# Correlation of pixels with their neighbours: the high parts multiplied in one direction, from a half-scaled tile that VectorE writes

## The reference, cut to what matters

```python
def conv_ref(feature, w, b):
    norm = sqrt(sum(feature * feature, axis=1, keepdims=True))
    fn = feature / maximum(norm, 1e-12)
    fp = pad(fn, 2 pixels of zeros on each side of H and W)
    sims = [sum(fp[:, :, r:r+32, c:c+32] * fn, axis=1) for c in range(5) for r in range(5)]
    cat = concatenate([feature, stack(sims, axis=1)], axis=1)      # 512 + 25 channels
    return relu(einsum('bihw,oi->bohw', cat, w) + b)

x = x + conv_ref(group_norm(x, 32 groups), w0, b0)
x = x + conv_ref(group_norm(x, 32 groups), w1, b1)
```

## Time and profile before

| | before |
|---|---|
| time, median of 3 runs (lowest to highest) | 539.54 us (538.83 to 540.25) |
| span of the profiled execution, first to last instruction | 538.4 us |
| own time of the profiled execution outside its span | not listed apart |
| busy: PE / PEld / DVE / ACT / POOL | 490.8 / 278.2 / 350.5 / 278.6 / 131.8 us |
| mean granted TensorE clock | 0.981 of full speed |

### The profile page before, as it was taken

How to read it: one execution, slowest core, us unless ns; L and a number is a source line. 1 busy time by engine, 2 the same in 40 slices (tenths; PEclk the granted TensorE clock), 3 DMA queues, 4 the chain that set the end, 5 groups by cost and what they waited for, 6 DMA issues and landing times.

```text
span 538.4 us, 7705 instructions
## 1 busy us (share of the span) xinstructions
PE 490.8 (91%) x2824; PEld 278.2 (52%) x2824; DVE 350.5 (65%) x820; ACT 278.6 (52%) x370; POOL 131.8 (24%) x189
## 2 busy tenths in 40 slices
PE   0658699489998999999999999999999999999996
PEld 0535355354644646464645556464646455564442
DVE  4788794767869296958758595858677676433322
ACT  1352544575394656647393757556473938433222
POOL 3453511040521313131220404040313112040400
PEclk9989799789999999999999999999999999999999
DMA  8282444441332716494957625042332326362332
GB/s 295 99 270 67 129 165 133 133 134 38 94 92 74 219 49 211 149 309 131 321 165 254 212 102 161 15 129 47 98 89 75 110 79 185 138 203 90 126 126 114
DMA packets 58547, 75.81 MB, mean 141 GB/s; under 512 B 11764, under 2 KB 45612, under 8 KB 58510
## 3 DMA queue, kind: packets, MB, share of 16 engines
q1 hardware_dynamic: 48718, 66.40, 36.7%
q0 software_dynamic: 9792, 8.92, 7.0%
HBM read 34.97 MB, written 37.79 MB: 135 GB/s over the span
## 4 chain that ended last, share of the span: by engine, by line
PE 77%; DVE 10%; ACT 4%; DMA 4%; POOL 2%; SPq 2%; issue 2%; DVEq 0%; ACTq 0%
PE conv_ps L530 56%; PE gram_ps L470 14%; PE conv_ps L539 5%; DVE stats L759 3%; POOL v L432 2%; DVE opnd L808 2%; DMA xs<-in_x_dram 1%; ACT opnd L627 1%; PE turn_ps L520 1%; ACT v L633 1%; DVE wmax L858 1%; ACT act_out L662 1%; DMA skew<-band_dram 1%; DMA band_dram<-band 1%; DVE xs L886 1%
## 5 line engine op out<-in xcount | busy, mean ns | idle before, releaser
L530 PE MATMUL conv_ps<-opnd,wh 128*128 128x512 f16 x512 | 194.9, 381 | 1.2 <-DVE wl L874 1.2
L530 PE MATMUL conv_ps<-opnd,whh 128*128 128x512 f16 x512 | 194.7, 380 | 0.0
L530 PE MATMUL conv_ps<-opnd,wl 128*128 128x512 f16 x512 | 194.7, 380 | 0.0
L662 ACT ACTIVATE act_out<-conv_ps,bias,wdown 128x512 f32<-128x512 f32 x128 | 96.4, 775 | 141.0 <-PE conv_ps L539 129.1
L886 DVE TENSOR_TENSOR xs<-xs,act_out 128x512 f32<-128x512 f32 x128 | 87.7, 696 | 50.8 <-ACT act_out L662 50.2
L470 PE MATMUL gram_ps<-opnd 128*128 128x256 f16 (+1 forms) x960 | 105.0, 269 | 3.4 <-ACT band L643 3.4
L470 PEld LDWEIGHTS gram_ps<-opnd 128*128 128x128 f16 x960 | 91.1, 100 | 16.6 <-ACT band L643 3.7
L808 DVE SCALAR_TENSOR_TENSOR opnd<-opnd,v 128x1024 f16<-128x1024 f16 x64 | 78.4, 1235 | 28.7 <-ACT v L633 21.3
L627 ACT ACTIVATE opnd<-xs,affine 128x1024 f16<-128x1024 f32 x64 | 78.8, 1238 | 17.4 <-DVE affine L802 17.4
L759 DVE BATCH_NORM_STATS2 stats<-xs 128x6 f32<-128x512 f32 x128 | 79.9, 681 | 5.6 <-DMA xs<-in_x_dram 5.6
L530 PEld LDWEIGHTS conv_ps<-opnd,whh 128*128 128x128 f16 x512 | 50.0, 98 | 61.2 <-issue 1.0
(11 more groups left out here) (77 smaller groups left out, 238.6 us busy)
## 6 DMA issues: line engine op xcount, KB each, us to landing
xs<-in_x_dram SPq DMA_DIRECT2D x32, 512.0 KB, 6.4
band_dram<-band SPq DMA_DIRECT2D x64, 256.0 KB, 2.9
out_dram<-xs SPq DMA_DIRECT2D x32, 512.0 KB, 2.9
skew<-band_dram SPq DMA_DIRECT2D x32, 266.0 KB, 3.5
vol<-corr_h POOLq DMA_DIRECT2D x48, 50.0 KB, 2.7
rows_dram<-rows SPq DMA_DIRECT2D x32, 65.8 KB
rows_dram<-rows SPq DMA_DIRECT2D x32, 63.3 KB
mirror<-rows_dram POOLq DMA_DIRECT2D x14, 110.9 KB, 2.6
```

What stands on the lines that cost most here:

```text
L530: pe.matmul(conv_ps[:, g % 4, :], w[:, l, t, m * P:(m + 1) * P], opnd[:, u % RING, part, t, n * HALF:(n + 1) * HALF], start=(t == 0 and w ...
L662: act.activation(act_out[:, g % 2, :], conv_ps[:, g % 4, :], ACT.Relu, bias=bias[:, l, m:m + 1], scale=wdown[:, l, m:m + 1]).then_inc(relu, 1)
```

## The change

The low part is kept single: the second pass writes v (`exact_tile`, `exact_tiles`), and DVE subtracts h from it. `whh` and `half_weights` are gone; the single low part meets `wh` in the convolution, and the doubling of the affine factors (L802) is gone. For the high parts, DVE writes a new tile `half` for each unit: for each block its own 128 columns times 0.5, and the 64 columns of the next two rows unscaled (`half_tile`: two instructions a tile, one of 8 x 128 and one of 7 x 64 f16 elements). PE multiplies a block's highs with these 192 columns (128 for the last block), while the lows still run over all rows from two above to two below; the mirrored sum supplies the rows above and the missing half. The order of the two parts in a sum is swapped, lows first. There is one `half`, so writing it waits until the products of the unit before are done (`gram`). The products wait for `halved` in place of `high`. In the slots the halves of tiles 0 and 1 stand behind low tile 1, those of tiles 2 and 3 directly behind their low tile; for unit 3 the first two stand behind `neighbours(2)`.

```diff
-        whh = sb("whh", [P, LAYERS, KT, C], F16)
-        v2 = sb("v2", [P, 2, PIX], F32)
+        v = sb("v", [P, 2, PIX], F32)
+        half = sb("half", [P, KT, BLOCKS, AHEAD], F16)      # AHEAD = (ROWS + R) * WI = 192
...
             def product(u, j, t, part):
                 p, h = j // 2, j % 2
-                r0 = max(ROWS * j - R, 0)
-                r1 = min(ROWS * (j + 1) + R, HI)
+                top = ROWS * j - (R if part else 0)
+                r0, r1 = max(top, 0), min(ROWS * (j + 1) + R, HI)
                 at = h * BAND + (r0 - (ROWS * j - R)) * WI
-                return pe.matmul(gram_at(u, p)[:, at:at + (r1 - r0) * WI],
-                                 opnd[:, u % RING, 0, t, j * P:(j + 1) * P],
-                                 opnd[:, u % RING, part, t, r0 * WI:r1 * WI],
-                                 start=(t == 0 and part == 0 and (u > 0 or h == 0)),
-                                 stop=(t == KT - 1 and part == 1 and (u > 0 or h == 1)))
+                size = (r1 - r0) * WI
+                moving = opnd[:, u % RING, 1, t, r0 * WI:r1 * WI] if part else half[:, t, j, 0:size]
+                return pe.matmul(gram_at(u, p)[:, at:at + size], opnd[:, u % RING, 0, t, j * P:(j + 1) * P], moving,
+                                 start=(t == 0 and part == 1 and (u > 0 or h == 0)),
+                                 stop=(t == KT - 1 and part == 0 and (u > 0 or h == 1)))
...
             def products(u, p):
                 if p == 0:
-                    pe.wait_ge(high, KT * (u + 1))
                     pe.wait_ge(low, KT * (u + 1))
+                    pe.wait_ge(halved, 2 * KT * (u + 1))
...
-                    for w, part in ((wh, 0), (wl, 0), (whh, 1)):
+                    for w, part in ((wh, 0), (wl, 0), (wh, 1)):
...
-                dve.wait_ge(gn_step, base + 10)
-                dve.tensor_scalar(affine[:, 1, :, :], affine[:, 0, :, :], 2.0, None, ALU.mult).then_inc(gn_step, 1)
...
             def low_tile(u, t):
                 dve.wait_ge(high, KT * u + t + 1)
-                dve.wait_ge(twice, KT * u + t + 1)
-                dve.scalar_tensor_tensor(out=opnd[:, u % RING, 1, t, :], in0=opnd[:, u % RING, 0, t, :], scalar=-2.0,
-                                         in1=v2[:, t % 2, :], op0=ALU.mult, op1=ALU.add).then_inc(low, 1)
+                dve.wait_ge(exact, KT * u + t + 1)
+                dve.tensor_tensor(opnd[:, u % RING, 1, t, :], v[:, t % 2, :], opnd[:, u % RING, 0, t, :], ALU.subtract
+                                  ).then_inc(low, 1)
+
+            def half_tile(u, t):
+                h = opnd[:, u % RING, 0, t, :].rearrange("p (j n) -> p j n", n=P)
+                wait(dve, gram, PAIRS * u)
+                dve.tensor_scalar(half[:, t, :, 0:P], h, 0.5, None, ALU.mult).then_inc(halved, 1)
+                dve.tensor_copy(half[:, t, 0:BLOCKS - 1, P:AHEAD], h[:, 1:BLOCKS, 0:AHEAD - P]).then_inc(halved, 1)
...
             for t in range(KT):
                 low_tile(0, t)
+                half_tile(0, t)
...
             low_tile(3, 1)
             correlation(1)
             neighbours(2)
+            half_tile(3, 0)
+            half_tile(3, 1)
             low_tile(3, 2)
+            half_tile(3, 2)
             low_tile(3, 3)
+            half_tile(3, 3)
...
                 if valid(k + 1):
                     low_tile(k + 1, 0)
                     low_tile(k + 1, 1)
+                    half_tile(k + 1, 0)
+                    half_tile(k + 1, 1)
                 for j in range(GROUPS):
...
                     if j in (1, 2) and valid(k + 1):
                         low_tile(k + 1, j + 1)
+                        half_tile(k + 1, j + 1)
```

More of the change, by code:

```diff
@@ L70, in build @@
     PAIRS = BLOCKS // 2
+    AHEAD = (ROWS + R) * WI
     REACH = 2 * R * WI + S
@@ L146, in build @@
         gtmp = sb("gtmp", [P, KT], F32)
-        affine = sb("affine", [P, 2, 2, KT], F32)
+        affine = sb("affine", [P, 2, KT], F32)
         nsq = sb("nsq", [P, BLOCKS], F32)
@@ L184, in build @@
         high = sem("high")
-        twice = sem("twice")
+        exact = sem("exact")
         low = sem("low")
+        halved = sem("halved")
         gram = sem("gram")
@@ L418, in scaled_weights, with exact_tiles @@
                                        ALU.mult, ALU.mult).then_inc(w_scaled, 1)
[L420 to L427, removed]
+            def exact_tiles(u, tiles):
                 pool.wait_ge(gn_step, GN_STEPS * (u + 1))
@@ L431, in double_tiles @@
                     wait(pool, low, KT * u + t - 1)
[L432 to L436, removed]
+                    pool.tensor_scalar(v[:, t % 2, :], xs[:, ring_slot(unit_batch(u)), t, :],
+                                       affine[:, 0, t:t + 1], affine[:, 1, t:t + 1], ALU.mult, ALU.add
+                                       ).then_inc(exact, 1)
+            exact_tiles(0, range(KT))
             scaled_weights(0)
-            half_weights(0)
-            double_tiles(1, range(KT))
+            exact_tiles(1, range(KT))
             volume_in(pool, 0)
-            double_tiles(2, range(KT))
+            exact_tiles(2, range(KT))
             volume_in(pool, 1)
             for k in range(EARLY, UNITS):
-                if k == W1_SLOT:
-                    half_weights(1)
                 views_from_dram(pool, k)
@@ L466, in product @@
                 p, h = j // 2, j % 2
[L467 to L468 removed]
+                top = ROWS * j - (R if part else 0)
+                r0, r1 = max(top, 0), min(ROWS * (j + 1) + R, HI)
                 at = h * BAND + (r0 - (ROWS * j - R)) * WI
[L470 to L474 removed]
+                size = (r1 - r0) * WI
[3 more added lines that the diff above has]
+                                 stop=(t == KT - 1 and part == 0 and (u > 0 or h == 1)))
             def first_products():
                 for t in range(KT):
[L479 removed]
                     pe.wait_ge(low, t + 1)
+                    pe.wait_ge(halved, 2 * (t + 1))
                     for p in range(PAIRS):
                         for j in (2 * p, 2 * p + 1):
[L483 removed]
+                            for part in (1, 0):
                                 last = product(0, j, t, part)
@@ L495, in products @@
                     for t in range(KT):
-                        for part in range(2):
+                        for part in (1, 0):
                             last = product(u, j, t, part)
@@ L528, in channels @@
                 for t in range(KT):
-                    for w, part in ((wh, 0), (wl, 0), (whh, 1)):
+                    for w, part in ((wh, 0), (wl, 0), (wh, 1)):
                         pe.matmul(conv_ps[:, g % 4, :], w[:, l, t, m * P:(m + 1) * P],
                                   opnd[:, u % RING, part, t, n * HALF:(n + 1) * HALF],
-                                  start=(t == 0 and w is wh), stop=False)
+                                  start=(t == 0 and w is wh and part == 0), stop=False)
             def volume(u, g):
@@ L593, in _ @@
                     u, g = job
-                    if u == TEAM and g == 0:
-                        pe.wait_ge(w_half, KT * LAYERS)
                     channels(u, g)
@@ L627, in norm_tile, with exact_tile @@
                 act.activation(opnd[:, u % RING, 0, t, :], xs[:, ring_slot(unit_batch(u)), t, :], ACT.Identity,
-                               bias=affine[:, 0, 1, t:t + 1], scale=affine[:, 0, 0, t:t + 1]).then_inc(high, 1)
-            def double_tile(u, t):
+                               bias=affine[:, 1, t:t + 1], scale=affine[:, 0, t:t + 1]).then_inc(high, 1)
+            def exact_tile(u, t):
                 wait(act, low, KT * u + t - 1)
-                act.activation(v2[:, t % 2, :], xs[:, ring_slot(unit_batch(u)), t, :], ACT.Identity,
-                               bias=affine[:, 1, 1, t:t + 1], scale=affine[:, 1, 0, t:t + 1]).then_inc(twice, 1)
+                act.activation(v[:, t % 2, :], xs[:, ring_slot(unit_batch(u)), t, :], ACT.Identity,
+                               bias=affine[:, 1, t:t + 1], scale=affine[:, 0, t:t + 1]).then_inc(exact, 1)
             def band_out_of_psum(u, p):
@@ L918, in _ @@
             low_tile(2, 2)
+            half_tile(2, 2)
             neighbours(1)
```

29 lines of the change are left out of this document (15 added, 14 removed).

## The result

Predicted were 544.5 us (range 536.5 to 552). The changed kernel takes 545.29 us (median of 4 runs, 544.88 to 548.47) where the kernel before, run beside it, takes 539.89: ratio 1.0118, 95% interval 1.0089 to 1.0147. It is slower by 1.2%, about as much as forecast. One caution: the profiled execution is the slowest of the four (548.47 us, span 546.7). The spans of the three others were 543.1 to 543.8, so what follows from its trace alone can be some 3 us too large.

The account below looks back on a forecast made before the run. PE was taken as the bound after about 175 us, DVE before, with a DVE-SP loop on slack in slots 5 to 9. 3.7 + 4.4 - 3.05 = +5.05 on span 538.4, plus 1.1: forecast 544.5 us, range 536.5 to 552.

Parts of the forecast that it names:

- PE's saving: Narrower highs of blocks 1 to 7 save 0.75 us a unit, 0.53 where PE is the bound and an average follows.
- The wait before pair 3: Sign: PE waits about 0.2 us in most slots for ACT to empty pair 1's bank, losing pair 2's 0.21 saving.
- The last part of the sum: From slot 10 on DVE recovers and PE is the bound: -0.2 - 4 x 0.53 - 0.75 = -3.05 us.
- The half tile: DVE's scaling of 1024 and copy of 448 f16 elements take 0.53 us a tile; four tiles 2.1 a unit.
- The rival of 0.9: A half tile costs 0.9 us on DVE, by L823's rate per element; 557 us in all; chance 0.10.
- The startup: Units 0 to 3 and slot 4: DVE's halves in line, less PE's savings and slot 4's gain, +3.7 us together.
- the gain foretold for slot 4: Halves mostly fill DVE's waits for ACT, and POOL no longer halves w1: -0.3 us.
- 1.9 + 1.9 + 0.8: Startup price of the halves: unit 0 +1.9 us, unit 1 +1.9, unit 3 +0.8, in line on DVE.
- Slots 5 to 9: Halves delay DVE's sums, SP's stores, loads and rows, and the next views; PE is +4.4 us at `average(11)`.
- each further slot adds about 1.6: In slots 5 to 9 DVE's lateness grows about 1.6 us a slot, less 0.3 to 0.7 in slots 6 and 7.
- DVE stays off the path after the startup: Rival: the loop of slots 5 to 9 gives way, PE keeps 6.05 us against 3.7: 537.2 us; chance 0.15.
- all hides: Rival: all added DVE work is hidden, 16 x 0.75 = 12 us off, 527.6 us; chance 0.03.

Follow-up runs that it names:

- pair 3 is free of ScalarE: Changed kernel with SyncE's stores and loads put off, plus ScalarE emptying pair 1's bank ahead of the average's square root: 535.23 us.
- the new order: Changed kernel, SyncE's stores of positions 2 and 3 and following loads put off behind the next slot's skewed reads: 536.01 us; kernel before likewise: 539.99.
- all three remedies: Changed kernel with SyncE's stores and loads put off, startup halves on ScalarE and in VectorE's wait, pair 1's bank emptied first from slot 5: 532.33 us.
- the run with ScalarE's halves: Changed kernel with SyncE's stores and loads put off, most halves of units 0 and 1 on ScalarE, two of unit 3 in VectorE's wait: 534.55 us.

## Why the prediction was right

*PE's saving: right, to 0.02.* 0.53 a slot was foretold, 0.51 is measured from slot 11 on, and 0.72 of the 0.75 once pair 3 is free of ScalarE (29.61 to 28.89). The wait before pair 3, foretold as 0.2, is 0.20 (0.28 less 0.08). The last part of the sum, -3.05 (its terms as written add up to -3.07), came out as -3.0. The unknown width of 128 columns costs no more than its columns: its step is 0.05 to 0.06 us (297.20 to 297.25), two thirds of the 0.0825 of 192 columns, so the 1.1 us kept for it were not needed.

*The half tile: right.* 0.54 us against 0.53. The rival of 0.9, by L823's elements, is out.

*The startup: the sum right, by luck in part.* +3.7 was foretold and +3.57 measured at `average(6)`. But up to the first volume matmul the profiled execution lost 2.5 us, where the text expected some 3.5, and the gain foretold for slot 4 is not what made it up. Between `average(3)` and `average(6)` the two kernels' waits and their stretches of lower clock fall in other places (granted clock 0.83 in 110 to 120 us before, 1.00 in 112 to 122 after; 1.00 in 142 to 152 before, 0.72 in 143 to 153 after), so slots 3 and 4 give and take 2 to 3 us. In slot 4 PE waited 1.17 us for pair 1's bank and 2.01 for the weights before; now it waits 3.40 for the bank and not for the weights, and the granted clock is 0.50 in the 4.5 us behind that wait:

```profile
148.52 0.39 PE L462 MATMUL gram_ps<-opnd 128*128 128x256 f16 x1 [3.40 <-ACT band L630]
```

That the sum of the startup came out within 0.13 us is luck. The halves' price there is better taken from the medians: 4.2 us, where 1.9 + 1.9 + 0.8 = 4.6 were foretold; units 0 and 1 bring 2.8 of it instead of 3.8. That DVE can't halve while POOL writes v is plain in the rows (1.26 against 0.41). The Trainium skill (SBUF — State Buffer, SBUF: two separate sides) describes it as an exclusive lock held for the whole instruction, and the trace agrees: POOL's two tiles end at 23.11, and the scaling that started at 22.13 ends at 23.39, 0.28 us behind them, when a free one takes 0.41.

*Slots 5 to 9: the mechanism right, its size too small.* PE waits where it was foretold, before `average(7)`, `turn(8)`, `turn(9)` and `average(9)` to `average(11)`. From slot 6 to slot 9 the views come every 32.0 to 32.3 us, beyond the 31 named as the sign; behind that the gaps are 26.0 and 27.8 us. That `average(7)` is 1.6 late at once is right as well: 20.70 against 19.11 us from the views of unit 4. The rest of its +5.77 is that these views come 4.18 late, and with that `turn(5)`, which the text left out, waits 1.57. DVE's own share is right too: +1.65 from views to sums, and the wait for ACT's root shrank to 0.28 us as foretold.

The step that was mis-sized is "each further slot adds about 1.6", which gave PE +4.4 at `average(11)`; it measured +7.72. DVE was to be late by 1.7, 3.0, 3.9, 5.2 and 6.6 us; counted from the views of unit 4, it was late by 1.7, 4.3, 5.4 and 7.6 at the views of units 5 to 8, and by 9.3 at `average(11)`. In slots 6 to 8 the way from the views to SP's rows takes 4.1 us more in all, where 3.5 were foretold. What was missing in this trace is mostly the landing of the rows, a leg that the text took as unchanged: POOL's request follows SP's rows by 7.80, 8.81 and 8.57 us, against 7.69, 7.53 and 7.87 before, +2.1 in all. The run without halves in units 0 and 1 shows how far that holds elsewhere: its slots are the same, and its profiled execution is at the median of its runs. There too the way to the rows is 4.1 us longer, but the rows reach POOL's request after 7.96, 7.67 and 7.94 us, only 0.5 more than before, and DVE is late by 8.1 us at `average(11)`, not 9.3. So some 1.2 us of the miss belong to the one execution, and some 1.5 stay.

That the order on SP's queue is what turns the halves into waits is shown: changed, it gives back 9.3 us in the changed kernel and nothing in the kernel before. Taking the halves out of the slots gives 8.0; so the new order gives back what they took and, by the medians, some 1.3 us more. That fits a part of PE's own saving, which the old order held back too (32.35 us up to `average(7)` without halves in the slots), but 1.3 us is little above the spread of the medians.

*The rivals.* That DVE stays off the path after the startup would have needed a loop that gives way; it did not, but the SP order shows what that is worth, 536.01 against the 537.2 worked out; the saving on PE, 6.0 against 6.05, fits, and the rest was worth some 2 us on that order, where 3.7 stood in the sum. That all hides, 527.6, ends at 532.33 even with all three remedies.

What stays open: where between the first volume matmul and the end the run with ScalarE's halves loses part of its 3.6 us, and why the rows behind the loads land at different times from execution to execution.

## What to carry to other kernels

A saving on the engine that sets the pace is only worth what the next loop leaves of it: look for the loops that live on slack (here sums, store and load issues, rows, views: 30.0 us against a slot of 29.6), and count every microsecond that the change adds to one of them once per turn. Work on a loaded engine need not become less to become free; it was enough to move the stores and loads out of the loop's way in the queue, and the test for the new place is what waits behind it there. Try such a reordering on the kernel before as well: where it gives nothing there, the change has made the loop the bound. And leave the added work out of the stretch once: here PE lost time there even without it.

## What the runs showed of the hardware

- Rows of 63 to 66 KB that SP issues right behind four loads of 512 KB reach POOL's request 7.5 to 9.1 us later (slots 4 and 6 to 8 of both kernels); with no load right in front, 4.32 to 4.35 in slots 5 and 9 of both, and 4.37 to 4.39 in slots 6 to 8 on the new order.
- DVE scales 1024 f16 elements a partition in 0.41 us and copies 448 in 0.28 (0.34 and 0.20 from start to start); ScalarE needs 1.04 and 0.56.
- Matmuls of 128 columns in f16, in turn with 192, take 0.05 to 0.06 us to the next start, those of 192 columns 0.08.
- After a wait of 3.64 us TensorE's granted clock read 0.50 in the following 2 us, and after one of 3.40 us 0.50 in the following 4.5. Where no later wait takes such a loss up, it stays: `average(6)` came 0.93 us later, though PE had left the wait 0.49 earlier than the run before (164.08 against 164.57).
